# ScalarE empties the count matrix two banks at a time, in place of one

## The reference

```python
def _sage_layer(x, src, dst, Wl, Wr, bias, n_nodes):
    msg_sum = jax.ops.segment_sum(x[src], dst, num_segments=n_nodes)
    cnt = jax.ops.segment_sum(jnp.ones((src.shape[0], 1), x.dtype), dst, num_segments=n_nodes)
    mean = msg_sum / jnp.maximum(cnt, 1.0)
    return mean @ Wl + x @ Wr + bias
...
for i in range(N_LAYERS - 1):
    x = _sage_layer(x, src, dst, W_agg[i], W_root[i], b[i], n)
    x = jax.nn.relu(x)
x = _sage_layer(x, src, dst, W_agg[-1], W_root[-1], b[-1], n)
```

## Time and profile before

| | us |
|---|---|
| median of 3 runs | 8128.8 (8126.4 to 8131.12) |
| the profiled execution | 8131.45 |
| its span, first to last instruction | 8129.1 |
| the stage of the adjacency steps | 2437 to 3445 of the span |

### The profile page before, as it was taken

The page is one execution under the profiler, slowest core; times in us unless marked ns, Lnnn a source line. Parts: engine busy times, 40 slices in busy tenths (PEclk is TensorE's granted clock), DMA queues, the critical chain, the costliest instruction groups (busy, mean ns, idle before and its releaser), DMA issues.

```text
span 8129.1 us, 101857 instructions
## 1 busy us (share of the span) xinstructions
PE 5028.7 (62%) x25982; PEld 3325.4 (41%) x25982; DVE 5111.2 (63%) x17152; ACT 2001.6 (25%) x3703; POOL 4896.4 (60%) x5045
## 2 busy tenths in 40 slices
PE   5566556666547777699999872542673533754532
PEld 3444443333334444354444442542443533434532
DVE  7777567777659898810001396853697843787744
ACT  6666654443416666610000000000100000000000
POOL 5777747777647777600000377777677776777774
PEclk8877777777767888799999855765656756556756
DMA  6555557777515555588888623421233321234311
GB/s 177 165 156 152 155 156 198 200 204 198 146 36 198 204 206 200 203 280 290 279 292 289 193 74 117 120 68 37 71 112 108 117 55 39 78 115 121 94 52 32
DMA packets 728900, 1216.85 MB, mean 150 GB/s; under 512 B 109340, under 2 KB 547085, under 8 KB 714832
## 3 DMA queue, kind: packets, MB, share of 16 engines
q1 hardware_dynamic: 552716, 847.76, 31.3%
q0 software_dynamic: 161120, 311.32, 14.7%
q10 hardware_dynamic: 14688, 53.48, 1.7%
HBM read 865.31 MB, written 346.85 MB: 149 GB/s over the span
## 4 chain that ended last, share of the span: by engine, by line
POOL 45%; PE 20%; issue 18%; DVE 14%; ACT 1%; DMA 1%; DVEq 1%; SPq 0%; POOLq 0%; ACTq 0%
POOL RO L1021 24%; POOL RO L980 18%; PE PS L1546 13%; PE PS L1501 3%; DVE H L2405 2%; DVE shared L2112 2%; POOL nd L1003 2%; DVE acc L1982 2%; DVE cut_row L2112 2%; DVE bn L2111 2%; PE PS L1481 1%; DVE RO L2393 1%; PE PS L1659 1%; POOL at_first L996 1%; DVE RO L1958 1%
## 5 line engine op out<-in xcount | busy, mean ns | idle before, releaser
L1021 POOL DMA_INDIRECT RO<-table,src_t x2346 | 2244.6, 957 | 2000.6 <-DMA table<-H 1244.4
L980 POOL DMA_INDIRECT RO<-table,src_t x2346 | 2309.3, 984 | 1021.0 <-issue 744.2
L1982 DVE TENSOR_TENSOR acc<-acc,PS 128x128 f32 x3910 | 1093.4, 280 | 1156.0 <-PE PS L1586 755.0
L1586 PE MATMUL PS<-RO 128*128 128x128 f32 x3060 | 683.4, 413 | 1174.7 <-DMA RO<-table,src_t 1151.1
L1586 PEld LDWEIGHTS PS<-RO 128*128 128x128 f32 x3060 | 631.4, 314 | 1219.2 <-DMA RO<-table,src_t 1196.7
L2211 DVE TENSOR_SCALAR RO<-PS,loc_t,shared 128x128 f32<-128x128 f32 x2346 | 940.4, 402 | 0.6
L1501 PE MATMUL PS<-RO 128*128 128x128 f32 x3128 | 623.4, 381 | 400.9 <-DMA RO<-table,src_t 386.3
L1501 PEld LDWEIGHTS PS<-RO 128*128 128x128 f32 x3128 | 599.8, 291 | 486.3 <-DMA RO<-table,src_t 461.5
L1286 ACT ACTIVATE small<-small 128x49 f32<-128x49 f32 x3 | 0.7, 245 | 2017.9 <-DVE small L2457 2017.9
L1146 ACT ACTIVATE H<-PS 128x392 f32<-128x392 f32 x784 | 392.4, 501 | 385.4 <-PE PS L1481 376.0
L1659 PEld LDWEIGHTS PS<-als_bf,RO 128*128 128x128 bf16 x7056 | 308.3, 119 | 426.8 <-DVE RO L2393 269.8
(11 more groups left out here) (403 smaller groups left out, 8833.3 us busy)
## 6 DMA issues: line engine op xcount, KB each, us to landing
GT<-adjacency SPq DMA_DIRECT2D x126, 1792.0 KB, 7.2
adjacency<-H SPq DMA_DIRECT2D x98, 1568.0 KB
RO<-adjacency SPq DMA_DIRECT2D x42, 1792.0 KB, 7.2
RO<-table,src_t POOLq DMA_INDIRECT x4692, 3.1
staged<-RO ACTq DMA_DIRECT2D x102, 512.0 KB
H<-staged SPq DMA_DIRECT2D x102, 512.0 KB
soft_rows<-shared SPq DMA_DIRECT2D x196, 256.0 KB
H<-soft_rows SPq DMA_DIRECT2D x98, 512.0 KB, 3.9
```

Source lines behind the costliest of these rows:

```text
L980: pool.indirect_dma_start(rows[:, h * HT + j, :], None, table[k % 2], at(src_t[:, t:t + 1]))\
L1021: pool.indirect_dma_start(rows[:, g % 2 * HT + j, :], None, table[k % 2], at(src_t[:, t:t + 1]))\
L1586: last = mm(PS[:, o:o + D], block[:, j * D:(j + 1) * D], onehot[:, h * HT + j, :], start=True, stop=True)
L1982: tt(at, at, window_at(k, c, j), ALU.add).then_inc(added[h], 1 if j < n - 1 else HT - n + 1)
```

## The change

In `evacuations` the loop skips the even windows. At each odd window `w` it waits until the steps of `w` are done, then copies the windows `w - 1` and `w` with one operation of 128 x 2 x 392 elements out of two neighbouring banks, and zeroes both with one operation, which raises `evacuated` by two. For the two windows of a pair to lie side by side, window `w` is now in bank `w % 4` instead of `(w + 1) % 4`, both here and in TensorE's step. The waits of TensorE and SyncE are written as before.

```diff
+                    if w % 2 == 0:
+                        continue
                     s.wait_ge(stepped, steps_done[w % LOAD_REGS])
-                    at = w % (2 * WN) // WN * SLAB_WORDS + w % WN * WN
-                    to = H[:, at:at + SLAB_WORDS].rearrange("p (h d) -> p h d", d=SLABW)[:, :, 0:WN]
-                    bank_of = (FIRST_BANK + (w + 1) % BANKS) * 512
-                    bank = PS[:, bank_of:bank_of + MASKW]
-                    nc.scalar.activation(to, bank.rearrange("p (h d) -> p h d", d=WN), ACT.Copy)
-                    nc.scalar.activation(bank, bank, ACT.Copy, scale=0.0).then_inc(evacuated, 1)
+                    at = w % (2 * WN) // WN * SLAB_WORDS
+                    to = H[:, at:at + SLAB_WORDS].rearrange("p (h d) -> p h d", d=SLABW)[:, :, w % WN * WN - WN:w % WN * WN + WN]\
+                        .rearrange("p h (b d) -> p b h d", d=WN)
+                    bank_of = (FIRST_BANK + (w - 1) % BANKS) * 512
+                    banks = PS[:, bank_of:bank_of + 1024].rearrange("p (b x) -> p b x", b=2)[:, :, 0:MASKW]
+                    nc.scalar.activation(to, banks.rearrange("p b (h d) -> p b h d", d=WN), ACT.Copy)
+                    nc.scalar.activation(banks, banks, ACT.Copy, scale=0.0).then_inc(evacuated, 2)
...
                 turn_of = window_of[i % LOAD_REGS]
-                bank_at = pe.snap(turn_of % BANKS * 512, min_val=0, max_val=(BANKS - 1) * 512)
+                bank_at = pe.snap((turn_of + BANKS - 1) % BANKS * 512, min_val=0, max_val=(BANKS - 1) * 512)
                 pe.wait_ge(evacuated, turn_of)
```

## The result

| | before | changed |
|---|---|---|
| median of 7 runs each | 8126.22 us | 8160.31 us |
| lowest and highest | 8119.86 to 8131.12 | 8147.68 to 8166.57 |
| ratio | | 1.0038, 95% interval 1.0027 to 1.0050 |

The account below looks back on a forecast made before the run. The loop of last mask, last step, window products and VectorE's first addition was taken to set a group's length. Late ends 15, slow loads 4 and tail 0.3 us gave 8149 us; range for 8 in 10: 8105 to 8200.

Parts of the forecast that it names:

- The bound: Stage where ScalarE empties the count matrix: TensorE waits for masks, never banks; the 67.0 us for zeroing are coincidence.
- ScalarE's relief: Copy and zeroing of a window pair take 1.44 us for 1.6; 60 us in all, worth nothing on the path.
- The release: Both banks of a pair come free 2.1 us behind the pair's last step, zeroing and signal included.
- The blocks: Burst behind the window products: TensorE steps wait 0.4 to 1.0 us for banks in nearly every group, then catch up.
- rival 2: Late steps at group ends are absorbed by waits for gathers or slow loads; 8125 to 8137 us; chance 0.22.
- rival 1: The blocked time of each burst is passed on, nothing caught up: 76 us, 8204 us; chance 0.20.
- The ends of groups: Late last steps delay the window products and VectorE; 1.9 us over eleven groups, +15 us for 89 groups.
- The slow loads: TensorE's register loads meet later slab stores: 0.3 us more for some 35 loads, perhaps 40% on the path, +4 us.
- The address term: One more term in each TensorE step's bank address stays inside its 0.09 us register operation: 0, at worst 32 us.
- What lies outside: Stretches before and behind the stage: untouched by the change, all other stages equal.

Follow-up runs that it names:

- the second profile: The changed kernel measured again with five further runs, on a chip where the kernel before takes 8127.98 us: 8160.75 us, ratio 1.004.

## Why the prediction was right, and where its sizes were off

The direction, the mechanism and the range were right; the loss is 34 us where 20 were forecast (8149 us). The stage took 1041 us where 1027 were forecast, and VectorE waited 129.0 us for the products where 110 to 125 were. Along the steps:

**The bound.** TensorE didn't wait for banks before: 5 of 780 openings stand close behind the zeroing that they need. The 67.0 us of the earlier trace rows were a coincidence, as said. The row's successor has 95.4 us and looks like more of the same, but now 154 of 390 openings stand right behind the zeroing that they need. The row can't tell the two apart; the records of which bank each step needs can.

**ScalarE's relief.** 821 and 822 ns where 820 was forecast, 0.72 us from copy to zeroing (2749.22, 2749.94), 644 us busy where 645 was forecast. It bought nothing: its idle time went from 376 to 476 us.

**The release.** 2.1 us behind the pair's last step was forecast; in the 154 held openings it is 2.10 us at least and 2.16 in the median, with the 0.19 us that the signal takes.

**The blocks.** One was forecast in nearly every group, 0.4 to 1.0 us long, five to ten steps in, to be caught up. They are in 86 of 89 groups, but 1.7 to a group, and in 54 of 154 more than ten steps of the group stand before them. The held steps stand 0.66 us (median) later than a step that follows closely (0.28 us) on the one before it, 101 us in sum; with the waiting for their own masks taken off it is 0.59 us, and 88 us in sum. At most the 33 us of the stage came of it, about a third, so neither is it all absorbed (rival 2) nor passed on in full (rival 1, whose 76 us took one block a group).

**The ends of groups: the term that was mis-sized.** I had walked eleven groups and found 1.9 us lost, 15 us for the stage. In these very groups the lag of the last step rose by 4.1 us in sum, which by 89/11 is 33 us, the whole growth. The sample was good, and the walk was not: it set each step against the timetable of before. In the group of the earlier trace rows it gave 0.71 us, and the lag rose by 1.25; in two groups whose ends have no block by such a walk the lag rose by 0.73 and 1.00 us. In both a second opening is held late in the group, the 14th step of 17 in one and the last in the other, behind a first one that is held at the 6th and the 9th. A block that arises because steps were shifted by an earlier one isn't in such a walk. In the second of these groups a register load has become slow as well (1.37 us for 0.59), so not all of its delay need be the banks'.

**The slow loads.** +4 us was forecast from later slab stores. Slow loads went from 49 to 70, the time in loads up by 12.6 us; at the 0.37 us of the small stores this is an estimate of 5 us. They aren't behind the late ends: the last load of a group is slow in 42 groups before and in 44 after, and the lag rose in either kind, from 1.83 to 2.14 us where it is slow and from 0.63 to 1.06 us where it is fast.

**The address term.** Taken as 0 with a bound of 32 us, because it "lies inside the register operation". It does, but that operation went from 90 to 100 ns, so 0 had no ground. With the nine uncovered steps of a group as in the prediction it is 89 x 9 x 0.01 = 8 us, an estimate; 1567 x 0.01 = 16 us is the most, and alone it costs nothing measurable (9448.27 against 9442.21 us, ratio 0.9998).

With 5 us of loads and 8 of the term some 20 of the 33 us are left to the release, where 15 were forecast. That steps are held by the late release is seen in every kernel that has it (56 to 272 held openings; in the kernels that free each bank by itself at most 7, or 62 with early loads). That it costs time rests on the pair's wait alone (+10 and +9 us, barely clear of the noise) and on the distance of 44 us with equal time in loads; no zeroing (-29 us in pairs, -14 with single banks) agrees. How the loss on the first chip divides between release, term and loads stays open, for those sizes are estimates, and so does why the distance was only 5.6 us with small stores. A mending that gives each bank back with its own zeroing behind the wide copy wasn't tried.

**What lies outside** was equal, 2437 and 4684 us in the second profile; in the first the work ahead took 11 us less, so a single execution can hide a third of the loss.

The rule quoted from the Trainium skill ("Perfetto Trace Analysis", Matmuls: let matmul groups rotate through banks so that the emptying of one overlaps the next) agrees with the trace here: with two units in rotation in place of four, 154 of 390 openings wait.

## What to carry to other kernels

Before two operations of an engine with idle time are merged, look at what they give back: a merged operation frees both buffers at the time of the later one, and the number of buffers that rotate is halved. Price it from the release time against the closest spacing of the consumers, not their mean, and carry each shift on into the next steps. A row that says "waited for the engine" proves a need for speed only if the event named is the one needed.

## What the runs showed of the hardware

- A register load of TensorE's sequencer out of SBUF takes 0.59 us, but mostly about 1.9 us while a 1568 KB store from SBUF is under way (49 of 196 loads before, all of them between 1.0 and 4.0 us behind the store's issue; none with a store of 32 KB).
- Loading 17 or 18 such values behind the products, ahead of their use, cost 177 us. The sequencer came to the loads 0.10 us behind the first product, but only 1.76 us of products were left, and the loads took 6.3 us from the first to the end of the last.
- One more term in a register expression costs 10 ns (90 to 100), although the number of instructions stays the same. It shows in full in the spacing of steps (274 to 284 ns) and in that from mask to step (291 to 301 ns).
- A zeroing on ScalarE lets a waiting step start 0.183 us after its end at the earliest without the term and 0.193 us with it.
- The same program took 8128, 9442 and 9501 us on three chips. The changed kernel was 0.4% slower on the first; without the address term, the form measured on the others, it was 0.12 and 0.18% slower there.
